# Output projection of self-attention: three passes of rounded operands instead of plain float32, and an earlier emptying of its bank

## What is computed

```python
def _attn(xq, xc, Wq, Wk, Wv, Wo, bo):          # xq = xc = layernorm(x)
    q, k, v = [(t @ W).reshape(B, 112, 16, 64) for t, W in ...]
    scores = einsum("bnhd,bshd->bhns", q, k) * 64 ** -0.5
    out = einsum("bhns,bshd->bnhd", softmax(scores), v).reshape(B, 112, 1024)
    return out @ Wo + bo                        # Wo: 1024 x 256
x = _attn(...) + x
```

## Time and profile before

| | us |
|---|---|
| median of three runs | 1719.04 (1717.07 to 1719.36) |
| the profiled execution | 1716.89 |
| its span | 1715.1 |
| TensorE matmul busy | 1579.0 (92% of the span) |
| VectorE busy | 1091.2 (64%) |
| ScalarE busy | 1004.3 (59%) |
| GpSimd busy | 265.8 (15%) |

### The profile page before, as it was taken

How to read it: one execution, slowest core, us unless ns; L and a number is a source line. 1 busy time by engine, 2 the same in 40 slices (tenths; PEclk the granted TensorE clock), 3 DMA queues, 4 the chain that set the end, 5 groups by cost and what they waited for, 6 DMA issues and landing times. The chain is left out here.

```text
span 1715.1 us, 37851 instructions
## 1 busy us (share of the span) xinstructions
PE 1579.0 (92%) x12042; PEld 1281.5 (75%) x12042; DVE 1091.2 (64%) x2548; ACT 1004.3 (59%) x2825; POOL 265.8 (15%) x502
## 2 busy tenths in 40 slices
PE   5999999699999999999999789969999999999787
PEld 4787777578878887888788678857777777777676
DVE  5546365657767666667677554457777777777543
ACT  3546364556546655565565443338778777777544
POOL 2001010231212112111312000011211122111000
PEclk9999999899999999999999999989999999999899
DMA  8000000020000000000000020000000000000000
GB/s 230 1 1 0 0 0 0 25 82 14 7 7 7 7 7 7 7 13 7 7 7 7 0 75 1 0 14 15 7 13 7 13 7 13 12 8 7 1 22 22
DMA packets 25244, 28.97 MB, mean 17 GB/s; under 512 B 1322, under 2 KB 23160, under 8 KB 24952
## 3 DMA queue, kind: packets, MB, share of 16 engines
q1 hardware_dynamic: 25208, 28.52, 5.6%
HBM read 26.68 MB, written 1.84 MB: 17 GB/s over the span
## 5 line engine op out<-in xcount | busy, mean ns | idle before, releaser
L788 ACT ACTIVATE B_probs<-banks,B_neg_max 112x375 f32<-112x375 f32 x256 | 144.7, 570 | 156.0 <-DVE B_neg_max L869 156.0
L1380 ACT ACTIVATE D_probs<-banks,D_neg_max 112x375 f32<-112x375 f32 x256 | 144.5, 570 | 76.5 <-DVE D_neg_max L1472 76.5
L869 DVE TENSOR_REDUCE B_neg_max<-banks 112x1 f32<-112x375 f32 x256 | 128.1, 542 | 94.1 <-PE banks L959 93.6
L1472 DVE TENSOR_REDUCE D_neg_max<-banks 112x1 f32<-112x375 f32 x256 | 128.0, 541 | 42.5 <-PE banks L1554 41.1
L625 PE MATMUL banks<-B_ctxT,B_wk_hi 128*128 128x378 f32 x390 | 123.0, 369 | 1.5 <-DVE B_wq_lo L858 1.5
L1387 ACT ACTIVATE D_probsT<-banks 126x336 f32<-126x336 f32 x262 | 104.1, 458 | 1.9 <-PE banks L1564 1.9
L985 PE MATMUL banks<-B_probsT,B_v 126*64 126x112 f32 x1584 | 105.0, 268 | 0.0
L877 DVE TENSOR_SCALAR B_probs<-B_probs,B_rsums 112x375 f32<-112x375 f32 x258 | 100.6, 432 | 4.6
L1480 DVE TENSOR_SCALAR D_probs<-D_probs,D_rsums 112x375 f32<-112x375 f32 x258 | 100.4, 431 | 4.6
L1578 PE MATMUL banks<-D_probsT,D_v 126*32 126x112 f32 x1584 | 101.5, 263 | 0.2 <-ACT D_probsT L1387 0.2
L762 POOL TENSOR_TENSOR B_q_hi<-B_q_group,ones 128x112 fp32r<-128x112 f32 x128 | 48.2, 377 | 339.4 <-PE banks L959 314.1
(11 more groups left out here) (297 smaller groups left out, 4087.1 us busy)
## 6 DMA issues: line engine op xcount, KB each, us to landing
ctx<-in_ctx_dram SPq DMA_DIRECT2D x34, 189.0 KB
ctx<-in_ctx_dram SPq DMA_DIRECT2D x34, 92.2 KB
w_stage<-in_L_xattn_Wq_dram SPq DMA_DIRECT2D x2, 1024.0 KB, 6.4
w_stage<-in_L_xattn_Wp_dram SPq DMA_DIRECT2D x1, 2048.0 KB, 8.0
w_stage<-in_L_xattn_W_dram SPq DMA_DIRECT2D x2, 1024.0 KB, 6.3
out_dram<-x_tokens SPq DMA_DIRECT2D x4, 448.0 KB, 3.3
x_tokens<-in_x_dram SPq DMA_DIRECT2D x1, 1344.0 KB, 16.7
w_stage<-in_L_xattn_Wk_dram SPq DMA_DIRECT2D x1, 1024.0 KB, 9.1
```

The costliest lines, as they stand in the source:

```text
L788: nc.scalar.activation(P[:, u % PS, j, 0:S], SB[j][0:N, 0:S], ACT.Exp, bias=nm[:, u % PS, j:j + 1], accum_out=sm[:, u % PS, j:j + 1]).then ...
L869: nc.vector.tensor_reduce(nm[:, u % PS, j:j + 1], SB[j][0:N, 0:S], AX.X, ALU.max, negate=True).then_inc(max_done, 1)
L1380: nc.scalar.activation(P[:, u % PS, j, 0:S], SB[j][0:N, 0:S], ACT.Exp, bias=nm[:, u % PS, j:j + 1], accum_out=sm[:, u % PS, j:j + 1]).then ...
L1472: nc.vector.tensor_reduce(nm[:, u % PS, j:j + 1], SB[j][0:N, 0:S], AX.X, ALU.max, negate=True).then_inc(max_done, 1)
```

## The change

- `wo` is split ahead of the loop into `woh` and `wol` by GpSimd: a product with ones that rounds, and a subtraction, 128 x 2048 each, behind the split of wv. TensorE waits for `wo_lo` where it waited for `wo_in`.
- oT becomes oTh and oTl. ScalarE's copy of bank OB writes the rounded oTh; a new function of VectorE, `o_rest`, subtracts oTh from bank OB into oTl, once per step. In steps 2 to 7 it stands behind `norm` and ahead of `maxima`.
- `project` issues twelve matmuls of rounded operands instead of four plain ones. `values` and `project` wait for VectorE's `o_lo` instead of ScalarE's `o_out`.
- `x_update` is cut in two. Its first part, `y_evac`, empties YB; it now stands ahead of `maxima` in steps 4 and 6. In step 7 and in the query and key part it stays behind what it was behind.

```diff
@@ tiles and semaphores
+        woh, wol = [sb(f"wo_{n}", [128, NP, D], F32R) for n in ("hi", "lo")]
-        oT = sb("oT", [128, NP, N])
+        oTh, oTl = [sb(f"oT_{n}", [128, NP, N], F32R) for n in ("hi", "lo")]
@@ gpsimd, behind wl[2]
+            pool.wait_ge(wo_in, 16)
+            flat = lambda w: w[:, :, :].rearrange("p t n -> p (t n)")
+            nc.gpsimd.tensor_tensor(flat(woh), flat(wo), k.ones[:, :].to_broadcast([128, NP * D]), ALU.mult).then_inc(wo_hi, 1)
+            pool.wait_ge(wo_hi, 1)
+            nc.gpsimd.tensor_tensor(flat(wol), flat(wo), f32(flat(woh)), ALU.subtract).then_inc(wo_lo, 1)
@@ scalar
-                nc.scalar.activation(oT[:, 4 * p:4 * p + 4, :].rearrange("p u n -> p (u n)"), OB[:, 0:4 * N], ACT.Copy
-                                     ).then_inc(o_out, 1)
+                nc.scalar.activation(oTh[:, 4 * p:4 * p + 4, :].rearrange("p u n -> p (u n)"), OB[:, 0:4 * N], ACT.Copy
+                                     ).then_inc(o_hi, 1)
@@ vector
-            def x_update(t):
+            def o_rest(i, p):
+                dve.wait_ge(o_hi, O0 + i + 1)
+                nc.vector.tensor_tensor(oTl[:, 4 * p:4 * p + 4, :].rearrange("p u n -> p (u n)"), OB[:, 0:4 * N],
+                                        f32(oTh[:, 4 * p:4 * p + 4, :]).rearrange("p u n -> p (u n)"), ALU.subtract
+                                        ).then_inc(o_lo, 1)
+
+            def y_evac(t):
                 dve.wait_ge(y_done, t + 1)
                 dve.wait_ge(x_done, t + X0)
                 nc.vector.tensor_tensor(tmp[:, :], YB[0:N, 0:D], k.bcast[:, 0, :], ALU.add).then_inc(y_out, 1)
+
+            def x_update(t):
                 dve.wait_ge(y_out, Y0 + t + 1)
...
                     keys(g, u)
                     if u == 0:
+                        o_rest(g * STEPS, 0)
                         pt_evac(g * STEPS)
+                    if u == 3:
+                        o_rest(g * STEPS + 1, 1)
                     if u == 6:
                         dve.wait_ge(k.rows_in, ROW_LOADS)
+                        y_evac(g * GB)
                         x_update(g * GB)
                 for s in range(STEPS):
                     i = g * STEPS + s
                     if s >= 2:
                         norm(i, (s - 1) % 2, 0)
                         norm(i, (s - 1) % 2, 1)
+                    if s >= 2:
+                        o_rest(i, s % 2)
+                    if s in (4, 6):
+                        y_evac(g * GB + (s - 1) // 2)
                     maxima(i, s % 2)
...
+                    if s == 7:
+                        y_evac(g * GB + 3)
                     if s in (4, 6, 7):
                         x_update(g * GB + (s - 1) // 2)
@@ vector, behind the loop
+            o_rest(NG * STEPS, 0)
             pt_evac(NG * STEPS)
+            o_rest(NG * STEPS + 1, 1)
+            y_evac(B)
             x_update(B)
@@ tensor
-                pe.wait_ge(o_out, i + O0 + 1)
+                pe.wait_ge(o_lo, i + O0 + 1)
                 if p == 0:
                     pe.wait_ge(y_out, t + Y0)
                 for u in range(4 * p, 4 * p + 4):
-                    ins = nc.tensor.matmul(YB[0:N, 0:D], oT[:, u, :], wo[:, u, :], start=(u == 0), stop=(u == NP - 1))
+                    nc.tensor.matmul(YB[0:N, 0:D], oTh[:, u, :], woh[:, u, :], start=(u == 0), stop=False)
+                    nc.tensor.matmul(YB[0:N, 0:D], oTh[:, u, :], wol[:, u, :], start=False, stop=False)
+                    ins = nc.tensor.matmul(YB[0:N, 0:D], oTl[:, u, :], woh[:, u, :], start=False, stop=(u == NP - 1))
...
                     if n == 5:
-                        pe.wait_ge(wo_in, 16)
+                        pe.wait_ge(wo_lo, 1)
```

More of the change, by code:

```diff
@@ L248, in self_attention @@
         OB, YB = k.bank[6], k.bank[7]
-        wo_in, w_hi, w_lo, wv_lo = sem("wo_in"), sem("w_hi"), sem("w_lo"), sem("wv_lo")
+        wo_in, wo_hi, wo_lo = sem("wo_in"), sem("wo_hi"), sem("wo_lo")
+        w_hi, w_lo, wv_lo = sem("w_hi"), sem("w_lo"), sem("wv_lo")
         gb_in, gb_turned, gb_set = sem("gain_shift_in"), sem("gain_shift_turned"), sem("gain_shift_set")
@@ L256, in self_attention @@
         rcp_done, norm_done, t_done = sem("rcp_done"), sem("norm_done"), sem("turned")
-        pt_act, pt_dve, av_done, o_out = sem("probsT_act"), sem("probsT_dve"), sem("av_done"), sem("oT_out")
+        pt_act, pt_dve, av_done = sem("probsT_act"), sem("probsT_dve"), sem("av_done")
+        o_hi, o_lo = sem("oT_hi"), sem("oT_lo")
         y_done, y_out, x_done = sem("y_done"), sem("y_out"), sem("x_done")
@@ L326, in _ @@
             act.sem_inc(exp_done, EXP0)
-            act.sem_inc(o_out, O0)
+            act.sem_inc(o_hi, O0)
             act.sem_inc(pt_act, PT0)
@@ L385, in _ @@
             dve.sem_inc(y_out, Y0)
+            dve.sem_inc(o_lo, O0)
             dve.sem_inc(x_done, X0)
@@ L515, in values @@
                 pe.wait_ge(pt_dve, PT0 + turned)
-                pe.wait_ge(o_out, i + O0)
+                pe.wait_ge(o_lo, i + O0)
                 for u in range(4):
@@ L569, in _ @@
                 pe.wait_ge(wv_lo, 1)
-                pe.wait_ge(o_out, first + 2 + O0)
+                pe.wait_ge(o_lo, first + 2 + O0)
                 pe.wait_ge(y_out, g * GB + Y0 + 1)
```

## The result

The changed kernel took 1725.15 us (median of 6, 1723.79 to 1727.18) against 1718.56 for the kernel before (median of 6, 1716.87 to 1719.36): ratio 1.0042, 95% interval 1.0029 to 1.0055. It is slower by 6.6 us; 1725.6 had been forecast. Its profiled execution has a span of 1722.9 us against 1715.1.

A forecast was written before the change was run, and what follows sets the result against it. A VectorE-ScalarE loop as long as TensorE's work was taken to bound the steps. Steady part +2.4 and start +4.2 gave +6.6: 1723.5 us profiled, 1725.6 on the runs' scale; own range 1722 to 1729, wider 1717.5 to 1732.

The forecast's parts named there:

- Loop of 4.70, and 0.54 for o_rest in it: Self-attention steps: a loop through VectorE and ScalarE takes 4.70 us, as long as TensorE's work; o_rest makes it 5.24.
- Distance by distance: Maxima into step 2, then step to step until 7: +0.50, +0.54, +0.90, -0.74, +1.26, -0.69; +1.77 us per group.
- Three passes 0.27 us cheaper per half projection: TensorE's projection: twelve rounded matmuls of 0.12 take 1.44 us against 1.71, saving 0.27 where TensorE is the limit.
- The drain of the last group at 0: End of self-attention: one more o_rest in series and an earlier start, taken as 0, between -1 and +1 us.
- Steady part: Self-attention behind the start: steps +7.1, three group ends -2.5, half projections among query-key products -2.2; +2.4 us.
- The start: GpSimd's rounding of wo delays VectorE's second normalisation, so TensorE's transposes (+3.1), and TensorE's clock may fall (+1.1): +4.2 us.
- the rival by which VectorE would be kept out: At the start, GpSimd leaves no gap and the normalisation waits for both halves of the split: 1731.8 us; chance 0.17.
- The wait for wo_lo: First projection: the split is ready by about 34 us, when TensorE is late itself, so this wait costs nothing.
- the rival's 8: In the steps, TensorE gets the lower clock: each takes 8 us or so, +60 us or more; chance 0.03.
- Two signs that came only in part: In the new trace: no wait of project() for attn_out, and a new wait of TensorE for o_rest.
- The faster one: TensorE sets the steps, so o_rest is hidden, stalls go and all 34 half projections gain: 1704.4 us; chance 0.08.
- The free start: The start costs nothing, if wo lands late or the stop is absorbed: 1721.4 us; chance 0.18.

The follow-up runs named there:

- experiment 1: The changed kernel with a second, useless 128 x 448 subtraction on VectorE behind each o_rest in steps 2 to 7; 1737.46 us (one run).
- experiment 2: The changed kernel without the pass oT_hi x wo_lo, eight matmuls per half projection in place of twelve; 1716.98 us (one run).
- experiment 5: The changed kernel with o_rest behind the maxima in steps 2 to 7; 1727.12 us, ratio 1.0047.
- experiment 7: The changed kernel with y_evac back behind the maxima, so three passes, o_rest and the split alone; 1736.93 us, ratio 1.0100.
- experiment 4: The changed kernel with wo rounded by ScalarE, behind the semaphore increments that open the other engines' loops; 1723.13 us, ratio 1.0030.
- experiment 6: The kernel before with only y_evac moved ahead of the maxima in steps 4 and 6, projection plain float32; 1708.51 us, ratio 0.9944.
- experiment 3: The changed kernel with wo rounded by ScalarE, ahead of the semaphore increments that open the other engines' loops; 1726.19 us, ratio 1.0045.
- experiment 8: The kernel before with each step's projection issued one step later, the last of a group behind it; 1718.46 us, ratio 1.0008.
- experiment 11: The kernel before with YB emptied between the two normalisations of steps 4 and 6; 1707.43 us, ratio 0.9933.
- experiment 9: The changed kernel with o_rest and y_evac behind the maxima, projections one step later, wo rounded by ScalarE behind the increments; 1715.10 us, ratio 0.9990.
- experiment 10: As experiment 9, with YB emptied between the two normalisations of steps 5 and 7; 1713.63 us, ratio 0.9965.

## Why the prediction held, point by point

- **Loop of 4.70, and 0.54 for o_rest in it.** Held: 5.24, and experiments 1 and 2 show that the loop is the one through VectorE: more for VectorE lengthens every step, less for TensorE shortens none.
- **Distance by distance.** Forecast 5.24, 5.60, 5.24, 6.55, 5.24; measured 5.24, 5.57, 5.24, 6.50, 5.23. (The terms given for the long one add up to 6.59 and not 6.55; that moves the sum by 0.2 us.) The first distance, into step 2, rose by 0.48 (forecast 0.50).
- **Three passes 0.27 us cheaper per half projection.** Twelve at 0.12, as forecast. The group's end with its two projections was to gain 0.84 + 0.54 = 1.38; the distance from step 7 to the next group's first maxima went from 30.42 to 29.05, 1.37.
- **The drain of the last group at 0.** From the last maxima to the last emptying 10.99 us against 11.07: - 0.1.
- **Steady part.** Forecast + 2.4, measured 5.65 - (3.63 at the first projection, 35.93 against 32.30) = + 2.0.
- **The start.** Forecast + 3.1 for the wait and + 1.1 for the clock. The wait was shorter: GpSimd's rounding took 3.67 us and not 4.2, the transposes came at 29.05 and not 29.65, and of these only the second half waited. So the first product behind the transposes came at 29.41 against 27.32, + 2.1. The clock cost more: the granted clock was 0.50 in 30 to 32 us, and the next two products took 33.49 - 29.41 = 4.08 against 29.85 - 27.32 = 2.53, + 1.55. Together 3.6 where 4.2 stood. VectorE did get in between two GpSimd instructions, as taken from L438. In this trace that is shown at 28.5; at 24.5 GpSimd stood idle for 0.27 us, waiting for wo. In those of experiments 1, 2 and 5 the rounding followed with no idle time, and VectorE got in there too: the rounding then took 3.98 us in place of 3.67. No trace shows the rival by which VectorE would be kept out.
- **The wait for wo_lo.** Costs nothing in this trace, as forecast: ready at 33.4, wanted at 35.7. That TensorE would be late by itself holds only while wo lands early enough for GpSimd to hold up VectorE; in the trace of experiment 7 it landed at 26.31 and the wait cost 2.19 us.
- **No fall of the clock in the steps.** Held for the changed kernel, where TensorE stops for at most 0.83 us. The margin is small: in experiment 1 the clock fell behind stops of 0.90 and 1.09 us, in experiment 7 behind 1.89. Even in experiment 7 the longest step took 7.27 us and not the rival's 8.
- **Two signs that came only in part.** project() still waits for attn_out, 2.9 us in eight pieces of at most 0.4, since it is now asked for ahead of the emptying's end; this is off the path of the maxima. And the new wait of TensorE's matmuls for o_rest comes once, behind the steps; in the steps TensorE waits earlier, for the probabilities.
- **The rivals.** The faster one needed TensorE to set the steps; experiment 2 took 0.49 us of its work away in each step and the distances stayed at 5.57 and 5.24. The free start needed the second normalisation at 0.6 us; it took 3.82, and 0.63 once the rounding was ScalarE's (experiment 4). Its other condition, a late wo, came about in experiment 7's trace, and the start was not free: the wait for wo_lo took the place of the other.
- **The total.** 1725.6 against 1725.15. The traced pieces that belong to the change are + 2.0 and + 3.6, 5.65 together where 6.6 stood. The two spans differ by 7.8 and the medians by 6.6, and the start of the cross-attention, 67 to 70 us whatever the kernel (last section), is enough for such differences. The terms are right in sign and near in size; that the totals agree to half a microsecond is partly luck.
- **What the prediction did not see.** It summed the change as one thing and treated the early emptying as 0.36 here and a stall gone there. Taken apart, it is two changes of opposite sign: the early emptying brings 10.0 us (experiment 6), the passes with o_rest and the split cost 17.8 on the plain kernel (7; 1736.93 - 1719.17) and 16.6 on the one of experiment 6 (1725.15 - 1708.51). The numbers for the first were all in the prediction (4.71, 5.06, 4.70, 5.29, 4.70 could be written down from the same rows), but it was not asked what half of the change would do.

## What to carry to other kernels

When an engine that works in order sits in a loop with another, price an added instruction by its place in that order, not by the engine's busy share: 0.54 us in the loop cost 0.54 each time, while the same engine idled 0.51 us two instructions earlier and took a 0.42 us instruction there for nothing. (Whether o_rest itself could stand there was not tried.) Look where each wait goes before moving work away from it: a projection one step later handed most of the stall from TensorE to VectorE, and the group's end paid for the rest. And price a change's parts one by one; the better half may be had alone.

## What the runs showed of the hardware

- A VectorE instruction with two SBUF inputs stood still for 3.2 us while GpSimd's 128 x 2048 TENSOR_TENSOR ran, and for 3.8 in the kernel before as well; o_rest (one input in PSUM) at 29.45 took 0.61 while GpSimd's next one ran from 28.59 to 33.40. The Trainium skill ("SBUF — State Buffer", section "SBUF: two separate sides") states that VectorE with two SBUF inputs and a GpSimd instruction that reads SBUF lock each other out for a whole instruction, and that the port pair VectorE has for itself never waits; these rows agree on both sides.
- Stops of TensorE of the same length don't cost the same, and a longer one can cost less. In the kernel before, TensorE stopped four times for 1.36 us in the steps, and its granted clock stayed at 1.00. In experiment 1 the clock fell to 0.50 behind one of four stops of 1.09 us and two of four of 0.90; in experiment 7 behind seven of eight of 1.89. At the start, the changed kernel and experiment 1 stopped nearly alike at the first transposes (1.57 and 1.41 us); the first maxima came at 54.13 in one and at 52.71 in the other, where the clock stayed up. What decides it no run here shows.
- The same in the drain: in experiments 3 and 4 the clock fell there, in the changed kernel it didn't, with the same instructions and the same idle times of TensorE (1.01 and 0.53 us) ahead of them.
- The same at the start of the cross-attention, where TensorE has little to do in every kernel (0.64 us of 5 in the earlier trace rows, 330 to 335). One window of each kernel, 18.4 us behind the last emptying in self-attention (after, at 331.24; before, at 325.59):

```profile
349.60:351.60 2.00, 1.50 (x4) 1.37 (x5) 1.89 (x5) 0.49 (x1) 1.92 (x2) 0.50 0.00 0
...
344.00:346.00 2.00, 1.55 (x8) 1.44 (x9) 2.00 (x6) 0.30 (x1) 1.92 (x2) 1.00 0.00 0
```

0.50 against 1.00: the granted clock is back in one and not yet in the other. From the last emptying in self-attention to the first in the cross-attention it took 67.1 us before and 69.0 after, in a program that is the same there. Of the other traces, 2, 7, 8 and 11 took 67.1 to 67.6 and 1, 3, 4, 5, 6, 9 and 10 took 68.8 to 70.0, so that both kinds of projection are found on both sides. The 1.9 us of difference between the two spans are therefore not counted as the change's doing. Why the clock comes back now earlier and now later is left open.
